# Issuing the wide half of the gathered adapter rows behind the third product of a main tile

## The reference

```
x = x + L0_ffn(L0_cond(x))
x = x + L1_ffn(L1_cond(x))
```

## Time and profile before

| | us |
|---|---|
| median of 3 runs (890.54 to 892.35) | 891.16 |
| the profiled execution's own time | 890.72 |
| its span, first to last instruction | 889.0 |
| TensorE busy | 883.4 |
| VectorE busy | 714.3 |
| ScalarE busy | 324.4 |
| GpSimd busy | 154.2 |
| mean granted TensorE clock | 0.999 |

### The profile page before, as it was taken

The page is one execution under the profiler, slowest core; times in us unless marked ns, Lnnn a source line. Parts: engine busy times, 40 slices in busy tenths (PEclk is TensorE's granted clock), DMA queues, the critical chain, the costliest instruction groups (busy, mean ns, idle before and its releaser), DMA issues.

```text
span 889.0 us, 13624 instructions
## 1 busy us (share of the span) xinstructions
PE 883.4 (99%) x4566; PEld 773.2 (87%) x4566; DVE 714.3 (80%) x1589; ACT 324.4 (36%) x525; POOL 154.2 (17%) x308
## 2 busy tenths in 40 slices
PE   9999999999999999999999999999999999999998
PEld 8999998888998888888888888888888888888887
DVE  6999999686787968999777877877877877877875
ACT  6588878421424424232322222222222222222221
POOL 0210020111011002313202212302302302302300
PEclk9999999999999999999999999999999999999999
DMA  9533340686312042575787987887887887987976
GB/s 344 214 94 120 125 137 24 231 274 191 99 49 95 3 140 77 176 280 205 231 284 254 297 295 254 294 298 252 297 284 258 299 287 258 300 293 252 303 245 222
DMA packets 62609, 191.93 MB, mean 216 GB/s; under 512 B 8256, under 2 KB 12742, under 8 KB 60620
## 3 DMA queue, kind: packets, MB, share of 16 engines
q1 hardware_dynamic: 50282, 158.92, 50.5%
q0 software_dynamic: 11968, 31.88, 12.9%
q10 hardware_dynamic: 290, 0.26, 0.1%
HBM read 158.80 MB, written 32.76 MB: 215 GB/s over the span
## 4 chain that ended last, share of the span: by engine, by line
PE 94%; DVE 3%; DMA 2%; ACT 0%; SPq 0%; issue 0%; DVEq 0%
PE bank L936 29%; PE bank L588 15%; PE bank L589 15%; PE bank L590 15%; PE bank L918 7%; PE bank L904 3%; PE bank L744 2%; PE bank L1045 2%; PE bank L913 1%; DMA t_lo<-t_scratch 1%; PE bank L632 1%; PE bank L853 1%; DMA m_raw<-m1t 1%; PE bank L639 1%; DVE t_lo L1494 1%; PE bank L870 0%
## 5 line engine op out<-in xcount | busy, mean ns | idle before, releaser
L936 PE MATMUL bank<-g_hi,xs 128*128 128x512 f32 x440 | 146.9, 395 | 0.0
L555 POOL DMA_DIRECT2D p1sel<-p_scratch x128 | 65.3, 510 | 290.9 <-issue 290.9
L936 PE MATMUL bank<-t_hi,xs 128*128 128x512 f32 x336 | 111.7, 392 | 0.4 <-DMA t_lo<-t_scratch 0.4
L936 PEld LDWEIGHTS bank<-g_hi,xs 128*128 128x128 f32 x440 | 81.6, 188 | 15.7
L936 PE MATMUL bank<-g_lo,xs 128*128 128x512 f32 x220 | 86.7, 394 | 0.0
L1122 ACT ACTIVATE xs<-x_raw 128x1024 fp32r<-128x1024 f32 x60 | 61.8, 1054 | 54.3 <-PE bank L936 52.6
L1494 DVE TENSOR_TENSOR xs<-x_raw,xs 128x1024 fp32r<-128x1024 f32 x60 | 73.5, 1247 | 8.3 <-ACT xs L1122 7.9
L588 PE MATMUL bank<-gx,xs 128*128 128x304 f32 x256 | 78.5, 307 | 0.0
L590 PE MATMUL bank<-gx,xs 128*128 128x304 f32 x256 | 77.4, 302 | 0.0
L589 PE MATMUL bank<-gx,xs 128*128 128x304 f32 x256 | 77.2, 302 | 0.0
L936 PEld LDWEIGHTS bank<-t_hi,xs 128*128 128x128 f32 x336 | 63.1, 188 | 15.0 <-DMA t_lo<-t_scratch 1.1
(11 more groups left out here) (395 smaller groups left out, 2119.3 us busy)
## 6 DMA issues: line engine op xcount, KB each, us to landing
t_hi<-t_scratch SPq DMA_DIRECT2D x82, 512.0 KB, 5.6
t_lo<-t_scratch SPq DMA_DIRECT2D x82, 512.0 KB, 6.6
x_raw<-xq SPq DMA_DIRECT2D x16, 1024.0 KB, 8.1
out<-ost SPq DMA_DIRECT2D x63, 256.0 KB, 7.9
p1sel<-p_scratch POOLq DMA_DIRECT2D x64, 192.0 KB, 5.8
w_raw<-wall SPq DMA_DIRECT2D x15, 512.0 KB, 4.6
w<-e_scratch SPq DMA_DIRECT2D x6, 1024.0 KB, 5.0
ea<-e_scratch POOLq DMA_DIRECT2D x8, 644.0 KB, 5.2
```

Source lines behind the costliest of these rows:

```text
L555: pool.dma_start(f(p1sel[b][64 * s:64 * s + STK, cs]), p1_dram[bass.ds(i * STK, STK), cs]).then_inc(sems[b], 16)
L936: mm = nc.tensor.matmul(bk[j][:], l[:, c, :], m[:, c, :], start=first and c + k == 0, stop=c + k == KH + 1, skip_group_check=True)
```

## The change

GpSimd's loop gets one more wait ahead of the wide transfers. In tiles 2 to 15 they are issued when the third product (position 24) of the tile that will use them has ended, instead of right behind the last low term of the tile before. Tiles 0 and 1 are as before.

```diff
@@ -577,6 +577,8 @@
                 load_p1(tau, ld_p1s, slice(D, NM1))
                 if tau:
                     pool.wait_ge(low_mm, tau)
+                if tau >= REG:
+                    pool.wait_ge(p6_mm, tau - REG + 1)
                 load_p1(tau, ld_p1w, slice(0, D))
```

## The result

The changed kernel takes 918.21 us (916.48 to 918.56, 4 runs) against 891.75 us (890.54 to 892.62, 4 runs): ratio 1.03, interval 1.0286 to 1.0314, slower by some 26.5 us. The profiled execution has a span of 916.7 us in place of 889.0.

A forecast was written before the change was run, and what follows sets the result against it. TensorE, busy 883.4 of 889.0 us, was taken to bound the kernel. Late copies (13 x 2.1 = 27.3 us) plus the last tile's 4.8 us made 32.1 us on 891.16: 923 us, forecast 915 to 931 (0.62), full range 904 to 938.

The forecast's parts named there:

- Nothing to win: Token part: TensorE waits only 0.4 us on transfers, so moving them gains 0, at most 0.4 us.
- The added wait: GpSimd, each tile: first wide issue 1.22 us behind product 24, the fourth starting 3.44 us after the first.
- The copies: GpSimd's eight copies for the next tile: begin 0.73 us behind the last issue, take some 4.4 us beside VectorE.
- The wait of TensorE: At x_product, on the late copies: 2.1 us a tile (bounds 0.5 and 3.2), 13 tiles, 27.3 us.
- The wide transfers in tiles 2 to 14: hidden: They land at 712.2 to 715.0 and are needed at 717.5, so they add no wait.
- The last tile: Low terms behind product 48 wait 4.8 us for the wide transfers (bounds 3.1 and 6.1), landing taken as 5.5 us.
- the second branch of rival 2: Matmuls at doubled pitch behind each stall: 1.8 us a tile, 24 us, total 947; rival 2 as a whole 0.16.
- The sum: Whole kernel: 27.3 + 4.8 = 32.1 us slower, 923 us on the median.

The follow-up runs named there:

- e6: The changed kernel, with VectorE's second half of x_low and the four sums waiting until the eight copies are done: 912.18 us, ratio 1.0236.
- e1: The changed kernel, with GpSimd making the eight copies for the next tile ahead of the added wait: 923.14 us, ratio 1.0361.
- e3: The changed kernel, with the eight copies ahead of the added wait and no added wait in tile 15: 913.59 us, ratio 1.0268.
- e8: The changed kernel, with the added wait moved to the middle of product 48, 4.3 us later: 992.19 us (2 runs).
- e2: The changed kernel without the added wait in tile 15: 910.52 us, ratio 1.0221.
- e5: The changed kernel, with the added wait on the second product and its m0 terms, 2.8 us earlier: 892.49 us, ratio 1.0015.
- e9: The changed kernel, with SP issuing the last tile's 2 MB load of t only when the wide transfers have landed: 913.59 us, ratio 1.0259.

## Why the prediction was right

Direction, place and mechanism were as forecast, and 918.21 lies in the forecast's own range (915 to 931), 5 us under the value. That it lies so near is in part luck: two terms were off in opposite directions, and one cover was thinner than I took it for. Step by step:

- *Nothing to win.* Right. TensorE had 0.4 us of transfer wait, and no run was clear of noise faster than before.
- *The added wait.* First issue 1.28 us behind product 24 (1.22 predicted), four issues in 3.44 us (3.44).
- *The copies.* Too dear by 0.9 us. They begin 0.22 us behind the last issue, not 0.73: I had read the gap between two issues as one that holds for any instruction. They take 4.04 us, not 4.4: the third pair waits out the subtraction as worked out, the fourth pair loses less. e6 shows the blocking by taking it away.
- *The wait of TensorE.* 1.26 us a tile in place of 2.1, with 0.15 us from the last copy to the matmul where I allowed 0.2. Twelve such tiles (1.26 to 1.4) and one of 4.7 make 20.2, 19.3 against the tiles of before, in place of 27.3. The 4.7 is no part of the forecast: a pause of 2.10 us ahead of an issue (the trace of before has one of 2.61 at no cost) is now on the chain, and 1.5 us of it are the lower clock.
- *The wide transfers in tiles 2 to 14: hidden.* Right for the changed kernel and by luck. I counted a landing by 715.0 and a need at 717.5. The fourth lands after 7.2 us, in the tile above at 728.3, where the low terms would want it at 724.80 + 3.44 = 728.24. It is the copies' wait of 1.26 that hides it. In the other tiles the fourth lands 5.3 to 7.6 us behind its issue, where 7.1 would be the limit without that wait, so that five of the thirteen needed the cover. I had the smaller margin in a half sentence, and took the cover for granted. e6 shows what is under it, and with the side effects named above e1 and e3 do as well: waits on the wide transfers, and on the load of t, which the forecast did not ask about in these tiles.
- *The last tile.* 4.8 us predicted for the wait, 6.45 measured: the landing was 7.1, not 5.5. I had taken the wide transfers of a quieter place and the narrow ones of this place, and it is a wide one at this place that was asked for. The 2.0 us of the lower clock are the second branch of rival 2, come true in the last tile, where I had said to look, and in one main tile (1.5 us), but not in the other twelve. The forecast itself had nothing for the clock. The Trainium skill's rule on long idle gaps (TensorE: Matmul & The Clock Gate, HAM oscillation — how this bites in real kernels) is borne out by the last tile (6.3 us) and by e8 (4.3 us and more); the waits of 1.0 us leave the clock alone, and one of 2.95 us did so in e2 but not in the changed kernel.
- *The sum.* 19.3 + 8.4 = 27.7 against 27.3 + 4.8 = 32.1. One term too large by 8.0, the other too small by 3.6.

## What to carry to other kernels

A wait added to an in-order queue is paid by what stands behind it: look for the strictest deadline among all of it, here eight small copies for the next tile and not the transfers that the edit names. Then ask what is due next, since removing the wait that the profile shows (16 us on the copies) may uncover another (in e6 6.8 us on the load of t) that it had hidden, and an edit that reorders the queue may add its own (16 us on transfers in e3). And a transfer's time to land belongs to its place among the other queues' loads, so take it from a transfer of that size in that place, or bound it from above.

## What was not expected of the hardware

- A transfer of 192 KB on GpSimd's queue lands in 2.9 to 3.6 us, and in 5.3 to 7.6 if it is issued at the start of a 2 MB load on SP's queue (changed kernel, 14 tiles). Its predecessor, 1.15 us earlier, is not touched, and neither is one issued 1.9 us ahead of the load (3.3 us, e5).
- GpSimd needs 0.65 us from the end of one issue to the next one, but only 0.22 us to a copy (0.53 in the one tile with the pause).
- TensorE's granted clock: 1.00 behind every wait of 1.0 to 1.9 us. Between 2 and 3.3 us it went both ways, even for one wait in one place: 1.00 behind 2.2 us (e9) and behind 2.95 (e2), but 0.50 a us behind 2.1 (e1), and 0.50 at once behind 2.95 in the changed kernel. 0.50 behind every wait of 4.3 us (e8) and more. Where it fell it cost 1.5 to 2 us.
- Delaying VectorE by a wait sped up the kernel by 6 us (e6), since its subtraction of x and its sums had held up GpSimd's copies (4.04 us for eight, 2.94 without them).
